# Moving the preparation of all weight scales and of the transformed output weights from ahead of the first batch to between its tiles, with weights stored tile by tile

## The reference

```python
xn = layernorm(x)
# branch 1, Mamba-2 with 16 heads of 64, state 128
zxbcdt = xn @ w_in                       # 512 -> 1024 z, 1280 xBC, 16 dt
xBC = silu(causal_conv4(xBC) + conv_b)   # x 1024, B 128, C 128
dt = softplus(dt + dt_bias)
y = ssd(x * dt, -exp(A_log) * dt, B, C) + x * D
y = rmsnorm(y * silu(z)) * norm_w
m = xn + y @ w_out                       # 1024 -> 512
# branch 2, gated feed-forward with a Walsh-Hadamard transform of length 2048
h = fwht(silu(xn @ W1.T) * (xn @ W3.T))  # 512 -> 2048
out = x + m + h @ W2.T                   # 2048 -> 512
```

## Time and profile before

| what | value |
|---|---|
| median of 3 runs | 1043.65 us (1041.88 to 1052.09) |
| profiled execution: time | 1048.69 us |
| profiled execution: span from first to last instruction | 1046.9 us |
| mean granted TensorE clock | 0.989 of full speed |
| PE busy | 923.5 us (88%) |
| DVE busy | 706.7 us (68%) |
| ACT busy | 381.2 us (36%) |
| POOL busy | 292.8 us (28%) |
| moved by DMA | 143.09 MB |

### The profile page before, as it was taken

One profiled execution on the slowest core, in us unless ns is written; L12 is line 12 of the kernel. 1 busy time (PEld: TensorE's weight loads), 2 busy tenths in 40 slices (PEclk: granted clock), 3 DMA queues, 4 the chain that ended last, 5 costly groups with the idle time before them and its releaser, 6 DMA issues.

```text
span 1046.9 us, 12960 instructions
## 1 busy us (share of the span) xinstructions
PE 923.5 (88%) x4892; PEld 462.9 (44%) x4894; DVE 706.7 (68%) x1032; ACT 381.2 (36%) x621; POOL 292.8 (28%) x182
## 2 busy tenths in 40 slices
PE   1027889887899999999999999999999999999997
PEld 1013334444454544555544444554544445554443
DVE  3997787888886175678774276677872565786741
ACT  3538456344342133523323234442321235323300
POOL 1962101333530020334520020444400111354300
PEclk9999999998899999999999999999999999999999
DMA  8438656643642153533622343642522433464122
GB/s 303 174 160 303 221 167 206 212 152 100 199 153 82 48 169 105 175 122 91 171 81 62 104 140 106 190 128 86 148 79 61 148 97 106 126 151 118 64 81 80
DMA packets 95102, 143.09 MB, mean 137 GB/s; under 512 B 7744, under 2 KB 46272, under 8 KB 91456
## 3 DMA queue, kind: packets, MB, share of 16 engines
q1 hardware_dynamic: 77120, 114.73, 35.1%
q10 hardware_dynamic: 17920, 27.53, 9.0%
HBM read 120.47 MB, written 21.76 MB: 136 GB/s over the span
## 4 chain that ended last, share of the span: by engine, by line
PE 63%; DVE 22%; DMA 5%; issue 4%; ACT 4%; SPq 1%; DVEq 0%; ACTq 0%
PE ps L431 39%; PE ps L585 16%; DVE arena L926 3%; PE ps L561 2%; DMA arena<-w_in 2%; DMA arena<-w1t 2%; DVE arena L344 2%; DVE arena L345 2%; PE ps L493 2%; DVE arena L949 1%; DVE arena L1044 1%; DVE arena L798 1%; PE ps L553 1%; ACT arena L689 1%; DVE arena L966 1%
## 5 line engine op out<-in xcount | busy, mean ns | idle before, releaser
L431 PE MATMUL ps<-xh,arena 128*128 128x512 f16 x1600 | 490.0, 381 | 24.0 <-DVE arena L966 9.2
L431 PE MATMUL ps<-xl,arena 128*128 128x512 f16 x800 | 305.0, 381 | 0.0
L431 PEld LDWEIGHTS ps<-xh,arena 128*128 128x128 f16 x1600 | 157.4, 98 | 217.8 <-issue 23.4
L1095 POOL TENSOR_TENSOR arena<-arena 128x512 f16<-128x512 f32 x64 | 77.9, 1219 | 323.8 <-ACT arena L729 323.8
L585 PE MATMUL ps<-arena 128*128 128x512 f16 x768 | 168.2, 379 | 0.0
L1101 POOL TENSOR_TENSOR arena<-arena 128x2048 f32<-128x2048 f32 x16 | 57.7, 3609 | 286.1 <-DMA arena<-cs_rows 286.1
L966 DVE SCALAR_TENSOR_TENSOR arena<-ps,cw,arena 128x511 f32<-128x511 f32 (+2 forms) x120 | 89.3, 746 | 51.0 <-ACT arena L719 49.2
L431 PEld LDWEIGHTS ps<-xl,arena 128*128 128x128 f16 x800 | 78.8, 98 | 89.8 <-issue 2.2
L585 PEld LDWEIGHTS ps<-arena 128*128 128x128 f16 x768 | 74.7, 98 | 88.7 <-issue 0.7
L729 ACT ACTIVATE arena<-arena 128x512 f16<-128x512 f32 x64 | 40.3, 630 | 166.5 <-DVE arena L987 166.5
L431 PE MATMUL ps<-wo_hi,arena 128*128 128x512 f16 x256 | 78.8, 379 | 4.9 <-DVE arena L1048 4.9
(11 more groups left out here) (148 smaller groups left out, 1173.4 us busy)
## 6 DMA issues: line engine op xcount, KB each, us to landing
arena<-w_parts SPq DMA_DIRECT2D x214, 256.0 KB, 2.6
w_parts<-arena SPq DMA_DIRECT2D x66, 256.0 KB, 2.4
arena<-cs_rows ACTq DMA_DIRECT2D x16, 1024.0 KB, 6.4
arena<-ecs_rows ACTq DMA_DIRECT2D x24, 256.0 KB, 7.5
arena<-w_in SPq DMA_DIRECT2D x4, 1160.0 KB, 17.4
arena<-w_in SPq DMA_DIRECT2D x18, 256.0 KB, 3.4
arena<-x SPq DMA_DIRECT2D x4, 1024.0 KB, 5.7
arena<-w2t SPq DMA_DIRECT2D x1, 4096.0 KB, 16.0
```

What stands on the lines that cost most here:

```text
L431: ins = nc.tensor.matmul(out_ap, lhs(i, a), rhs(i, c), start=(i == 0 and s == 0), stop=(i == n - 1 and s == 2))
L1095: nc.gpsimd.tensor_tensor(hid_lo[:, i, :], hs[i % 2], hid_hi[:, i, :], ALU.subtract).then_inc(hid_l.sem, 1)
```

## The change

The loop and its 50 tiles per batch stay. What stood ahead of the loop is gone except the layer norm and transposes of batch 0, and the scale and split of the first tiles. The rest becomes steps in a hand-written order for batch 0 (`FIRST`, then `STEP_FIRST`), which later batches don't have:

- `w_in` gets two scales: one for its first four tiles and the dt columns (IN0), one for the other fourteen (IN1). All 18 tiles of `w_in` are loaded once, into memory that later holds the hidden rows, and stay there until they are split. Step G1S, after the first tile, sums the norm of the second group.
- Steps K0 to K3 square a megabyte of W1 (ACT) and of W3 (POOL, in four pieces) and sum columns on PE; DVE takes the maximum per step. Step KS makes the scale.
- Steps F0 to F15 replace `butterfly`: a product in fp32 on PE with a 128x128 matrix that transforms groups of 16, copied out by ACT, and moved by a DMA inside the on-chip memory. Steps H0 to H15 are the second product (what L493 was), split by ACT and DVE, and stored. W2Q0 to W2Q3 square W2 on ACT; W2S makes its scale.
- WOL loads `w_out`, WOQ squares it on ACT, WOS makes the scale, WOH splits it on ACT and DVE.
- DT and SUM of batch 0 become steps in the list.
- A, U, C and Z weights arrive tile by tile in DRAM, 2 KB per partition in one run, written so by the host. W2 also has a layout of its own.
- The parameters and constants are now issued from ACT's queue, x of batch 0 in four pieces.
- In every batch G0 waits for the last tile to be read before its first bank, where it waited bank by bank; x of the next batch is loaded at a step XL (12 for batches 1 and 2, 20 for batch 0), where it was at A4.

```diff
+FIRST = ("B G1S C C0 DT C1 Z0 SUM C2 K0 Z1 C3 K1 Z2 W2Q0 F0 C4 F1 Z3 F2 C5 F3 K2 Z4 C6 K3 KS Z5 W2Q1 F4 C7 F5 "
+         "Z6 F6 Z7 F7 E0 A0 W2Q2 F8 F9 W2Q3 U0 F10 F11 A1 F12 F13 U1 F14 F15 W2S WOL A2 U2 H0 H1 H2 H3 A3 H4 H5 H6 H7 "
+         "U3 WOQ H8 H9 H10 H11 A4 H12 H13 H14 H15 U4").split()
+WO_AT = {"WOS": 11, "WOH": 12, "XL": 20}
+STEP_FIRST = {
+    "T": (10, 13, 19, 27),
+    "X": (10, 14, 20, 30),
+    "S": (12, 15, 22, 28),
+    "R": (13, 18, 25, 36),
+    "E": (None, 12, 16, 23),
+    "Y": (12, 17, 24, 33),
+    "Q": (12, 18, 26, 35),
+    "N": (14, 20, 28, 36),
+    "V": (14, 20, 29, 37),
+    "W": (17, 23, 31, 41),
+}
 STEP_AT = {
     "T": (3, 7, 17, 26),
     "X": (3, 11, 18, 29),
...
+        def load_ring(sp, n):
+            what, k = RING[n]
+            if n >= 4:
+                before, kb = RING[n - 4]
+                if before == "1":
+                    sp.wait_ge(k_act, kb + 1)
+                elif before == "3":
+                    sp.wait_ge(k_pool, 4 * (kb + 1))
+                else:
+                    sp.wait_ge(sq_w2, kb + 1)
+                    sp.wait_ge(f_done, 4 * (kb + 1))
...
+                    elif kind == "F":
+                        sp.wait_ge(f_out_ok, i + 1)
+                        sp.dma_start(resident[(i % 4) * 4 + i // 4::16], w2m[i % W2R]).then_inc(d_mid[i % W2R], 16)
...
+                    elif kind == "G1S":                                   # PE
+                        pe.wait_ge(scale_g0, 1)
+                        pe.wait_ge(sq_g1, len(G1_PIECES))
+                        pe_norm(pe, SQ_G1, SQ_G1 + 5, sum_g1)
+                    elif kind == "K":
+                        pe.wait_ge(scale_g1, 1)
+                        pe.wait_ge(ones16_ok, 1)
+                        if i > 0:
+                            pe.wait_ge(k_read, i)
+                        pe.wait_ge(k_act, i + 1)
...
+                        pe.wait_ge(k_pool, 4 * (i + 1))
...
+                    elif kind == "K":                                     # ACT
+                        n = RING_AT["1", i]
+                        act.wait_ge(d_ring[n % 4], 16 * (n // 4 + 1))
+                        if i == 0:
+                            act.wait_ge(sq_g1, len(G1_PIECES))
+                        else:
+                            act.wait_ge(k_sums, i)
+                        nc.scalar.activation(sq_act, ring[n % 4], ACT.Square).then_inc(k_act, 1)
...
+                    elif kind == "WOQ":
+                        act.wait_ge(d_wo, 16)
+                        act.wait_ge(f_done, 16)
+                        for q in range(QE):
+                            if q > 0:
+                                act.wait_ge(sq_wo, q)
+                            nc.scalar.activation(wo_junk, wo_raw[:, q, :], ACT.Square, scale=nw[:, q:q + 1],
+                                                 accum_out=row_sq[:, SQ_WO + q:SQ_WO + q + 1]).then_inc(sq_wo, 1)
...
+                    elif kind == "K":                                     # POOL
+                        n = RING_AT["3", i]
+                        pool.wait_ge(d_ring[n % 4], 16 * (n // 4 + 1))
+                        if i > 0:
+                            pool.wait_ge(k_sums, i)
+                        for s in range(4):
+                            piece = slice(s * TILE, (s + 1) * TILE)
+                            nc.gpsimd.tensor_tensor(sq_pool[:, piece], ring[n % 4][:, piece], ring[n % 4][:, piece],
+                                                    ALU.mult).then_inc(k_pool, 1)
```

More of the change, by code:

```diff
@@ L25 @@
 NT = MC + MZ + 2 * JF
[L26 removed]
+PARTS, W2R = 5, 4
 AHEAD = 3
@@ L51, with first_front, make_schedule @@
 PREP_AT = {"LN": 35, "XT": 40, "DT": 41, "SUM": 48}
-FRONT = "CZCCZCZCZCZCPCZCZCPZ"
-def make_schedule():
+def first_front():
+    tokens = []
+    for t in FIRST:
+        head = t.rstrip("0123456789")
+        i = int(t[len(head):] or 0)
+        if t in ("B", "C"):
+            tokens.append(("C", B_TILE if t == "B" else C_TILE))
+        elif t == "G1S":
+            tokens.append(("G1S", 0))
+        elif t == "W2S":
+            tokens.append(("W2S", 0))
+        elif t.startswith("W2Q"):
+            tokens.append(("W2Q", int(t[3:])))
+        else:
+            tokens.append((head, i))
+    return tokens
+def make_schedule(b):
     tiles = [(k, j) for j in range(JF) for k in "AU"] + [("G", j) for j in range(JF)]
-    convs, gates, pairs = [B_TILE, C_TILE] + list(range(QE)), list(range(MZ)), 0
+    convs, gates, n = list(CONV_ORDER), list(range(MZ)), 0
     seq = []
[L59 to L68, removed]
+    if b == 0:
+        seq = first_front()
+        n = sum(k in "AU" for k, _ in seq)
+    else:
+        for f in FRONT:
+            if f == "P":
+                seq += tiles[n:n + 2]
+                n += 2
+            else:
+                seq.append((f, (convs if f == "C" else gates).pop(0)))
+            if seq[-1] == ("C", C_TILE):
+                seq.append(("E", 0))
+    steps = [(at, 0, (kind, b + 1)) for kind, at in PREP_AT.items() if b + 1 < NB]
+    if b == 0:
+        steps += [(at, 0, (kind, 0)) for kind, at in WO_AT.items()]
+    elif b + 1 < NB:
+        steps.append((12, 0, ("XL", 0)))
+    steps += [(at, k, (kind, c)) for k, (kind, places) in enumerate((STEP_AT if b else STEP_FIRST).items(), 1)
               for c, at in enumerate(places) if at is not None]
-    n = 2 * pairs
     for at, _, item in sorted(steps):
@@ L167, in build @@
         yh, yl = cut(view(E // 2, FP16), QE), cut(view(E // 2, FP16), QE)
-        assert used[0] >= STAGED
-        raw = [cut(view(KD * P), KD) for _ in range(RAW)]
+        yl_end = used[0]
+        raw_at = used[0]
+        raw = [cut(view(KD * P), KD) for _ in range(2)]
         parts = [view(KD * P, FP16) for _ in range(PARTS)]
@@ L407, in _ @@
+            for n in range(4):
+                load_ring(sp, n)
+            store_parts(sp, 0)
+            for b in range(NB):
+                for kind, i in SCHEDULES[b]:
+                    if kind in WEIGHTS:
+                        p = POS[b][kind, i]
+                        if b == 0 and p + 1 < NT:
+                            store_parts(sp, p + 1)
+                        if b == 0 and N_FRONT <= p + AHEAD < NT:
                             load_raw(sp, p + AHEAD)
@@ new lines, in _, with split_lo @@
+            dve.wait_ge(steps.sem, k)
+            dve.nop().then_inc(scale_g0, 1)
+            dve_xl(dve, 0)
+            def split_lo(p):
+                dve.wait_ge(w_hi.sem, w_hi.at(0, p))
+                n = group(p)
+                nc.vector.scalar_tensor_tensor(out=part_lo[p % PARTS], in0=raw_tile(p), scalar=scl[:, n:n + 1],
+                                               in1=part_hi[p % PARTS], op0=ALU.mult, op1=ALU.subtract).then_inc(w_lo.sem, 1)
+            for p in range(AHEAD):
+                split_lo(p)
@@ L886, in _ @@
-            dve_xl(dve, 0)
-            dve.wait_ge(d_w2, 16)
-            for n in range(2):
-                butterfly(nc.vector, dve, n, 0, D_SPLIT, bf_dve)
-            dve.wait_ge(sums_w, 1)
-            to_scale(0, bank(3)[:, 0:KD], ALU.add)
-            steps.step(nc.vector.tensor_scalar(f_in[:], inv[:, 0:1], 1 / XS, None, ALU.mult))
-            k = steps.step(nc.vector.tensor_scalar(f_half[:], inv[:, 0:1], 0.5 / XS, None, ALU.mult))
-            dve.wait_ge(steps.sem, k)
-            dve.wait_ge(d_par, 16 * N_PAR)
```

766 lines of the change are left out of this document (418 added, 348 removed).

## The result

| | median | runs | ratio to before, 95% interval |
|---|---|---|---|
| before | 1046.01 us | 4 (1041.88 to 1052.09) | |
| after | 1123.42 us | 4 (1119.67 to 1127.76) | 1.0743 (1.0692 to 1.0794) |

The change made the kernel 77 us slower, where 16 us less were forecast. The profiled execution spans 1123.5 us.

What follows compares the result with a forecast made beforehand. PE was taken to bound the kernel from batch 1 on. Batch 0's G0 moves from 312.9 to 297 us (90 gained at the start, 74 given back), so 1043.65 - 16 = 1028 us, range 1000 to 1048.

Steps and rivals of the forecast that it cites:

- stretches 2 and 3: Batch 0 from the second tile to the column sums, 85 us, then ten tiles to T0, 55 us.
- After G0: Batch 0's step G0 onward: loads move within SP's list without a late one; the end is as before.
- the moves: DMAs inside the memory after F: the last hides under A2 and U2, at worst costing 3 us.
- stretch 4: Batch 0 from T0 to G0, 22 tiles: DVE 110 us plus 14 idle, 124 us (115 to 138).
- The first and second tile: Start of batch 0: first tile at 21 us instead of 110.9, second at 32, PE idle 6 us between.
- The terms of K: PE waits for ACT's eviction and square at K0 to K3: 3 us each, 5 at K0, 14 in sum.
- The clock term: Up to the end of the column sums, PE's gaps at K lower its clock: 0 to 8 us, 3 taken.
- POOL's squares beside DVE: POOL's squares of W3 block DVE's low splits: at most 1.2 us per collision, 0 to 19 us, 2 taken.
- WOQ: In the middle of H, ACT squares w_out in one 7.1 us piece and PE waits 7 us.
- Rival B: DVE and ACT bound batch 0 through compressed chunks, three gaps, 20 us in all; 1065 us (1050 to 1080), chance 0.15.
- The layout: Weight tiles in 2 KB runs: loads 2.6 instead of 3.4 us, 2 us less before G0.
- G0's wait: In batch 0, G0 waits for U15's read before its first bank: 1 to 1.5 us, once.

Runs made afterwards that it cites:

- Experiment 1: The changed kernel with SP issuing batch 0's streamed weight tile loads one tile earlier in its list (the lead): 1077.72 us, ratio to before 1.0335.
- experiment 6: The changed kernel with loads one tile earlier, and moves, H's stores and the load of w_out issued from ACT's queue (freed list): 1071.56 us, ratio 1.0275.
- experiment 4: The kernel before with one added wait: for 13 tiles of batch 0, SP loads tile p+3 only after DVE evicted tile p-1: 1073.55 us, ratio 1.0293.
- experiment 3: The changed kernel with the moves after F written over all 128 partitions instead of into eight (even moves): 1098.31 us, ratio 1.0538.
- experiment 11: The kernel of experiment 9 with the moves after F written over all 128 partitions instead of eight: 1049.52 us, ratio 1.0058.
- experiment 9: The kernel of experiment 6 with K's squares one tile earlier on ACT, WOQ spread behind H8 to H15, and WOH in eight pieces: 1059.35 us, ratio 1.0137.
- experiment 2: The changed kernel with the 16 moves after F issued from ACT's queue instead of SP's: 1090.00 us, ratio 1.0447.

## Why the prediction was wrong, point by point

**The step that failed** is the overlap of the loads in stretches 2 and 3, put at nothing in one sentence in "After G0": "The loads move within SP's list without a late one to be seen". I costed the F and H steps on PE, ACT, DVE and for the DMAs' own length, and never walked SP's list in order, although the moves and stores stand in it with waits of their own, between the loads. The sums of 85 and 55 us hold no term for it. Experiment 1 puts the order at 46 us of time and experiment 6 at 6 more; experiment 4 puts 29 us on one such wait with nothing else. This is the largest part of the miss, about 52 of 93 us (77 slower, 16 faster forecast), and with it alone the forecast would have said slower (1028 + 52 = 1080). It isn't all of it: with the list freed in full the kernel is still 27 us slower than before (1071.56 us, experiment 6), where 16 us less were forecast. Of the other 41 us the moves and stretch 4 are terms that were mis-sized, below; the rest stays open.

**The first and second tile** (21 and 32 us forecast) came at 24.0 and 33.8. ACT's first square waited for dt's weights until 11.8 us, where 9 to 10 was forecast, and a table load of 1.3 us stood ahead of it; from there on the steps took what was forecast.

**Stretch 2 up to the end of the column sums.** The terms of K were right in kind and in sum: 14 us forecast, 15.9 measured, PE released by ACT's square each time, in the changed kernel from 0 to 120 us:

```profile
PE ps L618 <- ACT arena L870: 15.9, 4, 7.8
```

K0 was the longest, 7.8 us instead of 5. ACT comes to its square at 59.8 us, behind DT and SUM and two table loads of 1.3 us (at 47.1 and 51.6); which of these makes it late wasn't separated. The clock term was small in the forecast (3 us) and isn't small in the trace: 0.90 granted over the stretch, 0.77 in the next one, 0.91 after it. In the next stretch the matmuls of a tile behind a gap of 5 to 7 us (147.8, 159.2, 171.2 us) start 0.43 us apart, the lower level of 1.2 GHz, and 0.22 us apart where the clock is back at 2.4 GHz. So the 81.5 us busy from 108 to 248.9 hold about 63 us of full-clock work (an estimate: 81.5 x 0.77). How much of it came back as time wasn't separated from the waits that caused it.

**POOL's squares beside DVE** cost little, as forecast (2 us): low splits that met them took 1.00 to 1.09 us instead of 0.75, one other operation 1.28 instead of 0.68 (103.2 us), none 4 us. Here is a split beside the first piece of K1's data, the squares in POOL's timeline (four in a row) and the split in DVE's, with one that met none:

```profile
65.56 4.48 POOL L1259 TENSOR_TENSOR arena<-arena 128x512 bf16<-128x512 f32 x4 [34.43 <-PE ps L623]
```

```profile
66.06 1.09 DVE L1059 SCALAR_TENSOR_TENSOR arena<-arena,scl 128x512 f16<-128x512 f32 x1
70.03 0.75 DVE L1059 SCALAR_TENSOR_TENSOR arena<-arena,scl 128x512 f16<-128x512 f32 x1 [0.44 <-ACT arena L798]
```

The four pieces keep the price of a meeting to 0.3 to 0.6 us here. The rule of the Trainium skill (SBUF — State Buffer, "Who interferes with whom"), by which the DVE instruction waits for the end of POOL's, agrees with the trace to about 0.3 us: the first piece ends near 66.7 us (an estimate, a quarter of 4.48 us behind 65.56), and 0.75 us of work behind that would end the split at 67.4; it ended at 67.15.

**WOQ** at 7 us was right: 7.5 us of wait in the changed kernel, 6.9 and 7.5 in experiments 1 and 6.

**The moves** were mis-sized. I took 3 us at worst. The median load took 4.9 us among them against 3.2 among even ones, and they cost 25 us inside the circle (experiment 3) and 10 us without it (experiment 11).

**Stretch 4** was forecast at 124 us and took 137.2, and 133.9 to 139.8 in the variants of the changed kernel (experiments 1 and 11 have the ends). I subtracted six tiles from both engines and let DVE's idle time shrink to 14 us; DVE was busy for 101.2 us, 9 less than forecast, and idle for 36. PE needed more than its 101 us too, 103.4 at a clock of 0.91. That the chain of the chunks doesn't shorten with the number of tiles is the reading that fits; no run isolates it. Rival B named this mechanism, with gaps at the compressed chunks (PE stood 7 us before the transposes of a chunk and 7.4 before a Y), and gave it 20 us; 13 came, and alone they would not have made the kernel slower. Rival B's sign was right, but not for its reason.

**The layout** was forecast at 2 us for its part; alone in the kernel before it gives 4.9 us (interval 2.8 to 7.8, worked out from the ratio). The forecast took the loads at a third shorter, and 2.6 for 3.4 us is a quarter; their medians moved by no more than 0.4 us. By the 512 bytes that the Trainium skill has as enough for full rate (DMA: Bandwidth & Descriptors, "Specifications") there would have been no gain; the runs side with a small one.

**G0's wait** for U15 was forecast at 1 to 1.5 us; it was 0.87 us, once.

So the miss at T0 is 77 us (248.9 for 172) and at G0 90 (386.1 for 296). Of the 77 the lead takes back 39 (T0 at 210.0), the freed list 10 more (199.9) and the even moves 8 (178.9 for 187.2). K and WOQ, whose removal brings T0 forward by another 11 us (188.7), are no part of the miss, since the forecast had charged 21 us for them. That leaves about 20 us at T0 that these runs don't assign, 2 of them the late second tile. Half clock is in it: in the trace of experiment 11 PE's busy time from 24 us to T0 exceeds full-clock work by some 9 us (an estimate: busy time times the share not granted, by stretch), and the forecast had 3. The other 13 us at G0 are stretch 4.

**What stays open.** Whether the chunks' chain in stretch 4 can be made shorter by another spacing of its steps wasn't tried, nor which of its links is the longest one. The 6 us that experiment 11 still lies behind the kernel before can't be assigned to one term by these runs. It lies 21 us behind the forecast's 1028, although about half of the waits that the forecast charged for K and WOQ are gone in it (10.4 us at K are left of 15.9, and the wait of 7.5 us behind WOQ is gone).

## What to carry to other kernels

Work that is spread between the tiles of a loop brings its DMAs with it. Before you cost the arithmetic, write down the list of the queue that issues them, with each wait, and ask of every load that another engine counts on: what now stands ahead of it, and does that depend on the very engine that will wait for the load? If it does, the lookahead is gone, however many buffers there are. The sign in this profile was a stretch in which no engine was busy for even 60% of the time and the queues for 43%. And the waits that go aren't the time that comes back: 52 us of them gave 46 us in experiment 1, the next 29 us only 6 in experiment 6.

## What the runs showed of the hardware

A load of 256 KB behind a DMA of 256 KB inside the on-chip memory from 128 partitions into eight took 4.9 us, and 6.7 to 6.9 behind two of them, in the chain of waits of the changed kernel from 118 to 180 us:

```profile
121.90 4.87 DMA arena<-w
150.21 6.71 DMA arena<-w
```

The same bytes into 128 partitions landed in 2.5 us and left the median load at 3.2 (experiment 3). As the volume and the queue are the same, the few target partitions made the price. With the moves on ACT's queue the median load on SP's took 3.3 us beside slow moves and 3.0 beside even ones (experiments 9 and 11), so there the loads paid little. It took 3.8 and 4.5 us in experiments 2 and 6, also with slow moves on ACT's queue; those weren't tried with even ones.
